# Splitting the value products by queries and issuing the transposed scores first in a two-layer gated cross-attention kernel

## The reference

```python
def reference(x, ctx_1024, g_xattn, g_ffn, ...):
    x = x + jnp.tanh(g_xattn[0]) * _L0_xattn_ref(_layernorm(x), ctx, ctx, Wq, bq, Wk, bk, Wv, bv, Wo, bo)
    x = x + jnp.tanh(g_ffn[0]) * _L0_ffn_ref(_layernorm(x), router_w, router_b, expert_weights)   # top 2 of 8
    x = x + jnp.tanh(g_xattn[1]) * _L1_xattn_ref(_layernorm(x), ctx, ctx, ...)
    x = x + jnp.tanh(g_ffn[1]) * _L1_ffn_ref(_layernorm(x), w1, w2)       # 256 -> 1024 -> gelu -> 256
    return x
# attention, per head:
    scores = jnp.einsum('bhqd,bhkd->bhqk', q, k) / sqrt(16)
    weights = jax.nn.softmax(scores, axis=-1)
    out = jnp.einsum('bhqk,bhkd->bhqd', weights, v)
```

## Time and profile before

| | |
|---|---|
| median of 3 executions | 766.89 us (765.59 to 769.69) |
| the profiled execution | 766.51 us |
| its span in the profile | 764.7 us |
| TensorE busy | 676.7 us (88%), 3550 matmul records |
| VectorE busy | 530.5 us (69%) |
| ScalarE busy | 446.8 us (58%) |
| GpSimd busy | 167.0 us (22%) |
| mean granted clock of TensorE | 0.96 of 2.4 GHz |

### The profile page before, as it was taken

How to read it: one execution, slowest core, us unless ns; L and a number is a source line. 1 busy time by engine, 2 the same in 40 slices (tenths; PEclk the granted TensorE clock), 3 DMA queues, 4 the chain that set the end, 5 groups by cost and what they waited for, 6 DMA issues and landing times.

```text
span 764.7 us, 10140 instructions
## 1 busy us (share of the span) xinstructions
PE 676.7 (88%) x3550; PEld 323.6 (42%) x3554; DVE 530.5 (69%) x1138; ACT 446.8 (58%) x572; POOL 167.0 (22%) x302
## 2 busy tenths in 40 slices
PE   4799999998999999998999989998889789987746
PEld 2433333344544445444554445443344344432324
DVE  3467876578886688868787688864786768775234
ACT  2227666773346633664336734468776778568746
POOL 6325222630010310121101410113210311021132
PEclk9769999999999999999999999999999999969987
DMA  7848578512120601123220321216032312200000
GB/s 239 230 117 317 180 232 267 158 34 52 42 43 29 166 18 26 46 108 84 43 43 30 122 47 42 43 70 207 10 83 64 94 39 64 43 2 9 21 0 28
DMA packets 39922, 66.74 MB, mean 87 GB/s; under 512 B 6080, under 2 KB 14784, under 8 KB 39616
## 3 DMA queue, kind: packets, MB, share of 16 engines
q1 hardware_dynamic: 39024, 65.57, 30.0%
q10 hardware_dynamic: 848, 0.53, 0.2%
HBM read 38.29 MB, written 27.26 MB: 86 GB/s over the span
## 4 chain that ended last, share of the span: by engine, by line
PE 56%; DVE 14%; ACT 12%; issue 9%; POOL 6%; DMA 2%; SPq 0%; POOLq 0%; DVEq 0%; ACTq 0%
PE psO L782 10%; PE psS L754 7%; PE psX L707 7%; DVE mx L1171 6%; PE psT L768 6%; PE psX L843 5%; PE psX L819 4%; ACT pt L991 4%; PE psX L844 4%; PE psX L845 4%; PE psX L727 3%; ACT qf L938 2%; DVE xs L1302 2%; POOL parts L574 2%; ACT parts L939 2%
## 5 line engine op out<-in xcount | busy, mean ns | idle before, releaser
L991 ACT ACTIVATE pt<-psT 128x1024 f32<-128x1024 f32 x256 | 261.8, 1023 | 217.1 <-PE psT L768 214.7
L1171 DVE TENSOR_REDUCE mx<-psS 128x1 f32<-128x512 f32 x512 | 325.1, 681 | 87.4 <-PE psS L754 86.1
L754 PE MATMUL psS<-ks,qs 48*128 48x512 f32 x512 | 153.8, 516 | 18.9 <-DVE mx L1171 13.2
L782 PE MATMUL psO<-pt,vg 128*32 128x512 f32 x1024 | 140.4, 621 | 0.1
L768 PE MATMUL psT<-qs,ks 50*128 50x512 f32 x512 | 118.2, 431 | 9.6 <-ACT pt L991 8.2
L754 PEld LDWEIGHTS psS<-ks,qs 48*128 48x128 f32 x512 | 61.0, 191 | 138.2 <-issue 72.3
L1302 DVE SCALAR_TENSOR_TENSOR xs<-psX,coef,xs 128x256 f32<-128x256 f32 x128 | 61.8, 483 | 31.8 <-PE psX L845 28.5
L574 POOL TENSOR_TENSOR parts<-qf,parts 128x512 fp32r<-128x512 f32 x32 | 40.8, 1275 | 158.7 <-ACT parts L939 158.7
L768 PEld LDWEIGHTS psT<-qs,ks 50*128 50x128 f32 x512 | 52.2, 189 | 29.4 <-ACT pt L991 25.8
L843 PE MATMUL psX<-moeh,xh 128*128 128x512 f32 x128 | 57.1, 446 | 5.3 <-DVE xs L1302 5.3
L844 PE MATMUL psX<-moel,xh 128*128 128x512 f32 x128 | 50.7, 396 | 0.0
(11 more groups left out here) (128 smaller groups left out, 748.9 us busy)
## 6 DMA issues: line engine op xcount, KB each, us to landing
ks<-kd SPq DMA_DIRECT2D x64, 192.0 KB, 3.7
qs<-qd SPq DMA_DIRECT2D x64, 192.0 KB, 4.5
kd<-parts SPq DMA_DIRECT2D x16, 512.0 KB, 3.1
qd<-parts SPq DMA_DIRECT2D x16, 512.0 KB, 2.7
kd<-parts SPq DMA_DIRECT2D x16, 256.0 KB, 3.8
qd<-parts SPq DMA_DIRECT2D x16, 256.0 KB, 3.7
ctxb<-in_ctxT SPq DMA_DIRECT2D x7, 512.0 KB, 3.5
xs<-in_x SPq DMA_DIRECT2D x4, 512.0 KB, 6.4
```

The lines of the kernel that those rows point to most:

```text
L754: mm(psS[:, i % 3, :], qs[at:at + KR, 2 * g + a, k * P:(k + 1) * P], ks[at:at + KR, 2 * g + a, :], start=True, stop=True).then_inc(pe_s, 1)
L782: i = mm(psO[32 * j:32 * j + 32, :], vg[:, p % 2, k, g * GH + j, :], pt[:, s % RING, j, :], start=k == 0, stop=k == NT - 1, tile_position= ...
L991: a(pt[:, G % RING, 2 * half:2 * half + 2, :], psT[:], ACT.Exp, scale=SCALE).then_inc(a_exp, 1)
L1171: v.tensor_reduce(mx[:, w // GH % 2, r, col:col + 1], psS[:, i % 3, :], AX.X, ALU.max).then_inc(v_max, 1)
```

## The change

- In each slot T is issued first, then half of the PV of the step before (256 of the 512 queries, all four heads), then S. For the first key tile of a group (k = 0) the PV is not halved; it is done in the second slot as before.
- The first two query projections are split by VectorE from PSUM, in one instruction, in place of a second ScalarE copy and GpSimd's subtraction.
- The maxima of a group go by two transfers instead of four, each over two partitions.
- BOB moves from the seventh last slot before slot 0 to the one before slot 0's own, later than most of the S of the head; the four BIAS of layer 0 move to slots 5, 13, 21 and 29 of piece 0.
- In the gelu burst the two V projections stand before and after the four F1 and no longer between them (pieces 5 and 6; piece 7 has none).
- In the tail new items BUSY issue 29, 4, 4 and 9 matmuls of 512 columns in bf16 whose results nobody reads.

```diff
-    put(lead, 24, ("BOB", ()))
-    put(lead, 25, ("BIAS", (0, 0)))
+    put(lead, 31, ("BOB", ()))
...
+    for b in range(B):
+        put(0, 5 + 8 * b, ("BIAS", (b, 0)))
...
-            for t in range(NT):
-                put(p, 16, ("F1", (t,)))
-                if p < NP - 1 and t in (1, 2):
-                    put(p, 16, ("VV", (p + 1, t - 1)))
+            burst = [("F1", (t,)) for t in range(NT)]
+            if p < NP - 1:
+                burst = [("VV", (p + 1, 0))] + burst + [("VV", (p + 1, 1))]
+            put(p, 16, *burst)
...
-    put(NP, 5, ("XQ", (0, 2)), ("LNN", (b, 2, 4)), ("XI", (0, 2)), ("XB", (0, 2)), ("XQ", (2, 4)), ("XI", (2, 4)))
-    put(NP, 5, ("F1", (0,)), ("XB", (2, 4)), ("F1", (1,)), ("F1", (2,)), ("F1", (3,)))
+    put(NP, 4, ("BUSY", (29,)))
+    put(NP, 5, ("XQ", (0, 2)), ("LNN", (b, 2, 4)), ("XI", (0, 2)), ("XB", (0, 2)), ("BUSY", (4,)), ("XQ", (2, 4)), ("XI", (2, 4)))
+    put(NP, 5, ("F1", (0,)), ("XB", (2, 4)), ("BUSY", (4,)), ("F1", (1,)), ("F1", (2,)), ("F1", (3,)),
+        ("BUSY", (9,)))
...
+        if 0 <= G < NP * H:
+            out.append(("T", (G, half)))
+        if 0 <= G - 1 < NP * H and (half or (G - 1) % GH):
+            out.append(("PV", (G - 1, half)))
         if 0 <= w < NP * H:
             out.append(("S", (w, half)))
-        if 0 <= G < NP * H:
-            out.append(("T", (G, half)))
-        if half == 1 and 0 <= G - 1 < NP * H:
-            out.append(("PV", (G - 1,)))
...
+        def by_dve(i):
+
+            return i in (split_no["Q", 0, 0], split_no["Q", 0, 1])
...
-                    for half in range(2):
-                        row, src = HALF * half + KR + k, k * GH * NT + half * 2 * NT
-                        sp.dma_start(qs[row:row + 1, 2 * g:2 * g + 2, :].bitcast(F32)
+                    sp.dma_start(qs[KR + k:HALF + KR + k + 1:HALF, 2 * g:2 * g + 2, :].bitcast(F32)
...
-            def pv_quad(s):
+            def pv_quad(s, half):
...
+                at = slice(half * S // 2, (half + 1) * S // 2) if k else slice(0, S)
                 for j in range(GH):
-                    i = mm(psO[32 * j:32 * j + 32, :], vg[:, p % 2, k, g * GH + j, :], pt[:, s % RING, j, :],
-                           start=k == 0, stop=k == NT - 1, tile_position=(0, 32 * j))
-                i.then_inc(pe_pv, 1)
+                    i = mm(psO[32 * j:32 * j + 32, at], vg[:, p % 2, k, g * GH + j, :], pt[:, s % RING, j, at],
+                           start=k == 0, stop=half == 1 and k == NT - 1, tile_position=(0, 32 * j))
+                if half:
+                    i.then_inc(pe_pv, 1)
...
+            def keep_busy(k):
...
+                for i in range(k):
+                    mm(psO[:], identb[:], w1q[:, 0, 0:S], start=True, stop=True)
...
+                v.scalar_tensor_tensor(out=parts[:, i % 2, 1, :].bitcast(F32R), in0=bank(), scalar=bqc[:, 0, c:c + 1],
+                                       in1=parts[:, i % 2, 0, :], op0=ALU.add, op1=ALU.subtract).then_inc(v_split, 1)
```

More of the change, by code:

```diff
@@ L103, in work_table @@
         st(0, 5 + t, 3, t)
-    put(0, 0, ("SPLIT", ("Q", 1, 0)), ("LD", ("x3",)), ("BIAS", (1, 0)))
+    put(0, 0, ("SPLIT", ("Q", 1, 0)), ("LD", ("x3",)))
     put(0, 1, ("LD", ("w1",)))
@@ L111, in work_table @@
     pair(0, 7, "XT", step=2)
-    put(0, 8, ("VV", (1, 0)), ("BIAS", (2, 0)), ("LD", ("moe0",)))
+    put(0, 8, ("VV", (1, 0)), ("LD", ("moe0",)))
     put(0, 9, ("ABS", (0,)), ("LNC", (3, 0, NT)))
@@ L118, in work_table @@
     put(0, 13, ("WS", ()))
-    put(0, 14, ("VV", (1, 1)), ("BIAS", (3, 0)))
+    put(0, 14, ("VV", (1, 1)))
     pair(0, 16, "SPLIT", "Q", 3, step=2)
@@ L218, in table @@
         w = G + LEAD
+        if 0 <= G < NP * H:
+            out.append(("T", (G, half)))
+        if 0 <= G - 1 < NP * H and (half or (G - 1) % GH):
+            out.append(("PV", (G - 1, half)))
         if 0 <= w < NP * H:
             out.append(("S", (w, half)))
[L221 to L226 removed]
+        if 0 <= G - 1 < NP * H and half == 1 and G % GH == 0:
+            out.append(("OE", ()))
         if half == 0 and G % GH == 1 and 1 < G <= NP * H + 1:
@@ L395, in build @@
         v_xn = sem("v_xn")
+        v_split = sem("v_split")
         v_norm = sem("v_norm")
@@ L426, in build, with dve_parts, pool_parts, act_parts @@
                 split_no[args] = len(split_no)
+        def by_dve(i):
+            return i in (split_no["Q", 0, 0], split_no["Q", 0, 1])
+        def dve_parts(i):
+            return sum(by_dve(k) for k in range(i))
+        def pool_parts(i):
+            return i - dve_parts(i)
+        def act_parts(i):
+            return 2 * i - dve_parts(i)
         def ctx_of(p):
@@ L692, in split @@
                 l = p // B
+                i = n("SPLIT")
+                b = n.piece() % 2
                 o = bank("SPLIT")
+                last[b] = (v_split, dve_parts(i + 1)) if by_dve(i) else (a_split, act_parts(i + 1))
                 if what == "Q":
@@ L1128, in vv, with split @@
                                 ALU.add).then_inc(v_vv, 1)
+            def split(what, p, c):
+                i = n("SPLIT")
+                if not by_dve(i):
+                    return
+                if due(pe_split, i + 1):
+                    dve.wait_ge(pe_split, i + 1)
+                if due(a_split, act_parts(i + 1)):
+                    dve.wait_ge(a_split, act_parts(i + 1))
+                v.scalar_tensor_tensor(out=parts[:, i % 2, 1, :].bitcast(F32R), in0=bank(), scalar=bqc[:, 0, c:c + 1],
+                                       in1=parts[:, i % 2, 0, :], op0=ALU.add, op1=ALU.subtract).then_inc(v_split, 1)
             def raw(k):
@@ L1354, in f2 @@
                                        in1=xs[:, b, t, :], op0=ALU.mult, op1=ALU.add).then_inc(v_f2, 1)
-            walk({"BOB": scale_bo, "ST": stats, "LNV": normalise, "VV": vv, "ABS": abs_sum, "WS": scales, "QUANT": quant, "S": maxima,
+            walk({"BOB": scale_bo, "ST": stats, "LNV": normalise, "SPLIT": split, "VV": vv, "ABS": abs_sum, "WS": scales, "QUANT": quant, "S": maxima,
                   "NT": norm, "OP": op, "R1": router1, "R2": router2, "R3": router3, "R4": router4, "ME": experts, "XQ": xq,
```

41 lines of the change are left out of this document (26 added, 15 removed).

## The result

The changed kernel takes 808.23 us in the median against 768.29 of the kernel before in the same comparison: a ratio of 1.0506 (95% interval 1.0469 to 1.0542), 5% slower. One of its four executions took 884.86 us at a mean granted clock of 0.726 and does not count in the ratio. Its span in the profile is 806.0 us, its mean granted clock 0.955. The forecast was 797.5 us, 758 to 815.

What follows compares the result with a forecast made beforehand. TensorE was taken as the bound: 56% of the chain, little idle time in pieces 1 to 4. Against 766.5 us, -1.7 + 11 + 21 + 8 - 4.4 - 2.9 = +31.0 gave 797.5 us, range 758 to 815.

Steps and rivals of the forecast that it cites:

- head -1.7: Before piece 0: VectorE's split, later BOB and fewer transfers save 1.7 us, between 0 and -3.
- piece 0 +11: Piece 0: half PV and second S fall behind the waiting T, costing 11 us, between +4 and +14.
- pieces 1 to 4 +21: Pieces 1 to 4: extra blocks add 26 us, idle time absorbs 5; +21, between +10 and +33.
- pieces 5 to 7 +8: Pieces 5 to 7 up to the last burst: 14 to 21 us more work, partly absorbed; +8, between 0 and +17.
- 4.4 for the bursts: Gelu bursts of pieces 6 and 5: moved V projections save 2.2 us each, -4.4, between -2 and -5.2.
- tail -2.9: Tail: BUSY keeps the clock up, speeding F1, transposes and F2; -2.9 us, between 0 and -4.
- The price of T, half PV and S apart: Each step with work in both slots: T 0.43, half PV 0.57, S 0.43; 0.52 us more per step.
- The first rival: Whole kernel: weights load ahead, so separating T and S costs nothing; 757.5 us, chance 0.15.
- e as a constant of every block: TensorE everywhere: each block of matmuls in one array shape costs 0.21 us besides its columns.
- The share of idle time that takes something up: Pieces 1 to 4: a third of TensorE's 16.2 us of idle time, 5 us, absorbs added work.
- The loop through ScalarE: Piece 0: T waits 2.44 us behind a projection for ScalarE's exponential; step grows from 4.78 to 5.78 us.
- the 2.2 that the prediction gave TensorE: Gelu bursts: ScalarE gains 2.6 us, TensorE a little less, 2.2 us, for each of two bursts.

Runs made afterwards that it cites:

- foreign block: Kernel with old order, whole PV and only the smaller changes, plus an 8-column full-shape matmul between S and T: 817.67 us; same-shape control 780.89 us.
- the halves by themselves: Kernel before, in its old order, with PV in halves of the queries: 778.48 us, ratio 1.0137.
- the moves alone: Changed kernel with the old order and whole PV, leaving only the smaller changes at head, gelu burst and tail: 764.48 us, ratio 0.9958.
- the new order from piece 5 on: Changed kernel with its order and halved PV starting only at piece 5, the old order in pieces 0 to 4: 772.73 us, ratio 1.0060.

## Why the prediction was right, and where it was off

Measured in one execution each, forecast beside it: head -1.7 forecast, 0.0 found; piece 0 +11 and +9.5; pieces 1 to 4 +21 and +23.2; pieces 5 to 7 +8 less 4.4 for the bursts, that is +3.6, and +11.1 found (the pieces' +8.6 without the tail's -2.5); tail -2.9 and -2.5. The sum is +31.0 against +41.3. The time lies in the range, nearer to its upper end than to the middle.

**The price of T, half PV and S apart** was right to a hundredth: 0.43, 0.57, 0.44. The first rival, that weights load ahead and the boundaries cost nothing, fell with these rows, with the weight loads that start together with their matmuls, and with S at 0.44 and T at 0.43 around a foreign block. What was wrong in the derivation is e as a constant of every block: the small foreign block cost 0.11.

**Pieces 1 to 4.** The share of idle time that takes something up, a third, was right in sum: +21 forecast, and 5.0 in piece 2, the one at full clock before and after, which is 20 for four. The 10 us more at the lower clock in the others can account for the rest of the +23.2. How the share splits the prediction had not seen: the halves by themselves are taken up whole in pieces 3 and 4, and the separation is paid.

**Piece 0.** The loop through ScalarE was read rightly: 5.78 forecast and 5.78 found per step. The term came out 1.5 too high.

**Pieces 5 to 7** hold the term that failed, the -4.4 for the bursts. From the first T of piece 5 to the last copy of `psO` the kernel before takes 237.9 us, the one with the moves alone 238.1, the one with the new order from piece 5 on 246.3 and the changed kernel 249.0; at 1.2 GHz they are for 17, 24, 20 and 31 us of it. So the bursts gave nothing (+0.2), the order with the halves cost 8.2 where +8 was forecast, and the last 2.7 go with 10 us more at the lower clock. Of the 7.5 us by which the forecast of this part was too low, the bursts are 4.6.

ScalarE's bursts did shrink by 2.6 us, as forecast. What became of it is read from T to T in piece 6, the kernel with the moves alone first and the kernel before second:

```profile
607.39:611.23 3.84, 3.84 (x20) 1.66 (x22) 0.81 (x2) 2.54 (x3) 0.60 (x2) 0.56 0.98 239
611.23:621.32 10.09, 9.69 (x50) 5.13 (x48) 3.88 (x7) 9.46 (x10) 0.00 (x0) 1.00 0.42 109
...
605.50:608.35 2.85, 2.41 (x21) 1.02 (x21) 0.81 (x2) 2.20 (x3) 0.61 (x2) 1.00 0.97 218
608.35:620.71 12.36, 9.51 (x49) 5.35 (x48) 4.47 (x7) 9.68 (x10) 0.00 (x0) 1.00 0.47 143
```

The stretch with the burst takes 10.09 us in place of 12.36, so the 2.2 that the prediction gave TensorE are there. They are given back on both sides of it: 1.0 in the half step ahead, at a granted clock of 0.56 in place of 1.00, 0.5 behind it at full clock (2.46 us in place of 1.96), and 0.75 in the half step after that, at 0.70 in place of 1.00. The 0.5 is S waiting for VectorE's maximum, first with the moves alone, then before:

```profile
623.78 0.49 PE L778 MATMUL psS<-ks,qs 48*128 48x512 f32 x1 [0.87 <-DVE mx L1217]
...
622.67 0.50 PE L754 MATMUL psS<-ks,qs 48*128 48x512 f32 x1 [0.32 <-DVE mx L1171]
```

The prediction counted ScalarE's gain as the piece's and did not ask what TensorE meets behind the burst. It had no term for the clock either. Why the grant falls in other places there stays open; no kernel here changed it alone.

**The head.** The prediction priced the new VectorE instruction and did not ask what is queued behind it. VectorE's timeline after:

```profile
21.89 0.75 DVE L1173 SCALAR_TENSOR_TENSOR parts<-psX,bqc,parts 128x512 fp32r<-128x512 f32 x1 [6.29 <-ACT parts L974]
22.56 0.42 DVE L1135 BATCH_NORM_STATS2 st<-xs 128x6 f32<-128x256 f32 x1
```

It idles for 6.29 us in front of the split, with the statistics of the second batch behind it; before, they were done in that gap, by 16.7. Layer norm, transposes and the first S follow late: S starts at 31.02 where it had started at 29.61, 1.4 us later and not 1 us earlier. TensorE's projection of 5.14 us in place of 3.67, partly at 1.2 GHz, adds to it. BOB's place wins 0.5 of this back by the time of the group's transpose (42.23 against 41.33), the rest is won behind it, where the two transfers are, and the first T starts at 46.1 as before. That an ST ahead of the split would cure it wasn't tried.

**The tail.** BUSY does what it was read to do:

```profile
777.75 6.21 PE L932 MATMUL psO<-w1q,identb 128*128 128x512 bf16 x28
785.13 0.38 PE L884 MATMUL psX<-identb,xi 128*128 128x128 bf16 x4 [1.17 <-ACT xi L1056]
...
786.21 1.03 PE L905 MATMUL psT<-w1q,xit 128*128 128x512 bf16 x4
```

These 29 matmuls (28 are recorded) end 1.17 us before the transpose's input is there, F1 takes 1.03 in place of 1.86, and the tail from the last copy of `psO` is 36.1 us in place of 38.6. In the other kernels with BUSY the profiled tail is 36.0 to 38.4 us, in those without it 38.3 to 39.1, so the gain is not the same in every one.

**Is it all the clock?** No. The changed kernel has 72.0 us at 1.2 GHz and the kernel before 61.4; the 10.6 us between them cost at most 5.3 of the 41.3. An execution of the changed kernel with a mean clock of 0.962 took 804.2 us; the executions of the kernel before at 0.962, a dozen over all comparisons, took 765.5 to 767.8. The clock does decide a few us from one execution to the next: the kernel with the moves alone runs from 758.6 at 0.968 to 767.5 at 0.962.

## What to carry to other kernels

Where TensorE works without gaps, count the changes of array shape per round before reordering: two pairs of row-tiled matmuls of 512 columns cost 0.67 us side by side and 0.87 apart, and half of a column-tiled product cost 0.57 of a whole one's 1.00. Splitting the value products evenly over the half steps gave nothing here, since TensorE was not short of work. A shorter burst on one engine did not shorten its piece here: what is gained has to be followed to the half steps on both sides of it. When an instruction moves to an engine that works in order, ask first what stands behind it while it waits: twice here, at the head and in piece 0, that cost more than the instruction saved.

## What the runs showed of the hardware that was not expected

A matmul of 8 columns between two row-tiled pairs costs more than its columns even in their own shape: 0.17 us, against 0.11 plus the separation's 0.20 in the full shape. A weight load starts 0.23 us ahead of its matmul beside a neighbour of the same shape (378.18 for 378.41) and together with it behind one of another shape (398.57 for both). The granted clock can stay at 0.50 with TensorE busy for 3.84 to 4.00 us of every 4 from 30 to 54 us of one execution, while another of the same kernel has a mean clock of 0.980.
